# The scaling of row maxima to biases, moved from ScalarE to GpSimd in 29 of 32 head pairs

## What is computed

```python
h = _layernorm(x, axis=-1) * (1 + ca) + sa
x = x + ga * _L0_attn_ref(h, wq, wk, wv, wo)
h = _layernorm(x, axis=-1) * (1 + cb) + sb
x = x + gb * _L0_ffn_ref(h, W_base, b_base, W_gate, W_thr, b_thr, A_w, B_w)
```

```python
scores = jnp.einsum('bqhd,bkhd->bhqk', q, k) * scale
scores = jnp.where(causal[None, None], scores, jnp.finfo(scores.dtype).min)
probs = jax.nn.softmax(scores, axis=-1)
out = jnp.einsum('bhqk,bkhd->bqhd', probs, v).reshape(b, s, d)
```

## Time and profile before

| | us |
|---|---|
| median of 3 runs | 1601.21 (1600.83 to 1603.35) |
| the profiled execution | 1600.5 |
| its span | 1598.7 |
| granted TensorE clock over the span | 0.987 of 2.4 GHz |
| TensorE busy | 1539.8 |
| ScalarE busy | 1039.8 |
| VectorE busy | 934.7 |
| GpSimd busy | 605.6 |

### The profile page before, as it was taken

One profiled execution on the slowest core, in us unless ns is written; L12 is line 12 of the kernel. 1 busy time (PEld: TensorE's weight loads), 2 busy tenths in 40 slices (PEclk: granted clock), 3 DMA queues, 4 the chain that ended last, 5 costly groups with the idle time before them and its releaser, 6 DMA issues. The chain is left out here.

```text
span 1598.7 us, 29576 instructions
## 1 busy us (share of the span) xinstructions
PE 1539.8 (96%) x9578; PEld 1209.3 (76%) x9578; DVE 934.7 (58%) x2900; ACT 1039.8 (65%) x2718; POOL 605.6 (38%) x477
## 2 busy tenths in 40 slices
PE   5899999999999999999999999998989999999996
PEld 3667777777777777777777777775669989999996
DVE  4727576576665656666657566666654545454544
ACT  2548899999999988999899899988631111110100
POOL 3334253443533324235243243337114343434342
PEclk9999999999999999999999999997999999999999
DMA  9783444445542393243333432444341212122110
GB/s 344 273 261 86 107 108 108 123 114 142 131 117 74 86 304 83 66 99 74 95 74 81 107 81 61 97 143 120 120 119 40 79 41 77 50 70 63 55 66 27
DMA packets 172035, 174.44 MB, mean 109 GB/s; under 512 B 21044, under 2 KB 120676, under 8 KB 171896
## 3 DMA queue, kind: packets, MB, share of 16 engines
q1 hardware_dynamic: 169784, 168.54, 38.0%
q10 hardware_dynamic: 2112, 4.19, 0.7%
HBM read 96.65 MB, written 25.18 MB: 76 GB/s over the span
## 5 line engine op out<-in xcount | busy, mean ns | idle before, releaser
L1584 ACT ACTIVATE rows_sb<-rows_sb,bias_m 128x640 f32<-128x640 f32 (+7 forms) x512 | 396.0, 774 | 12.5
L1854 DVE CUSTOM_DVE_ANT_0 rows_sb<-ps_t,mask 128x512 f32<-128x512 f32 (+3 forms) x512 | 297.4, 586 | 162.7 <-PE ps_t L1313 155.5
L1313 PE MATMUL ps_t<-stk 96*128 96x512 f32 (+3 forms) x768 | 268.6, 352 | 5.1 <-DMA stk<-rot 1.7
L1620 ACT ACTIVATE probsT<-ps_s 128x512 f32<-128x512 f32 (+1 forms) x488 | 243.2, 536 | 33.3 <-PE ps_s L1344 17.3
L1344 PE MATMUL ps_s<-stk 98*128 98x512 f32 (+3 forms) x768 | 222.7, 371 | 1.0 <-DMA stk<-m_rows 1.0
L1880 DVE TENSOR_TENSOR ps_s<-ps_s,mask_t 128x128 f32<-128x128 f32 (+1 forms) x384 | 120.8, 341 | 166.3 <-PE ps_s L1344 162.7
L1313 PEld LDWEIGHTS ps_t<-stk 96*128 96x128 f32 x768 | 146.0, 190 | 51.9 <-DVE m_rows L1870 9.6
L2016 POOL TENSOR_TENSOR rope_b<-rope_b,rope_sin 128x512 f32<-128x512 f32 x64 | 82.8, 1293 | 267.6 <-DVE rope_b L1839 267.6
L1344 PEld LDWEIGHTS ps_s<-stk 98*128 98x128 f32 x768 | 132.2, 191 | 66.4 <-issue 30.2
L1854 DVE CUSTOM_DVE_ANT_0 rows_sb<-ps_t,mask,smax_part 128x128 f32<-128x128 f32 (+3 forms) x256 | 140.8, 550 | 39.4 <-PE ps_t L1313 11.9
L1300 PE MATMUL ps_qkv<-hT_hi,w_hi 128*128 128x512 f32 x384 | 158.2, 412 | 3.9 <-DVE hT_lo L1823 3.9
(11 more groups left out here) (222 smaller groups left out, 3179.8 us busy)
## 6 DMA issues: line engine op xcount, KB each, us to landing
stk<-rot SPq DMA_DIRECT2D x384, 128.0 KB, 2.4
probsT<-in_L_wmod_dram SPq DMA_DIRECT2D x5, 2048.0 KB, 9.0
wm_one<-in_L_wmod_dram SPq DMA_DIRECT2D x5, 2048.0 KB, 11.5
w_raw<-in_L_attn_wq_dram SPq DMA_DIRECT2D x16, 512.0 KB, 3.9
w_raw<-in_L_attn_wk_dram SPq DMA_DIRECT2D x16, 512.0 KB, 4.7
w_raw<-in_L_attn_wv_dram SPq DMA_DIRECT2D x16, 512.0 KB, 4.1
attn_scratch<-attn_sb SPq DMA_DIRECT2D x128, 64.0 KB, 3.0
h_scratch<-h_pair SPq DMA_DIRECT2D x32, 256.0 KB, 3.1
```

Of the source, the lines that this page charges most:

```text
L1313: pe.matmul(bank[:, 0:c1 - c0], stk[0:3 * HD, u % 2, 0, qt // 4, h, qt % 4 * P:(qt % 4 + 1) * P], stk[0:3 * HD, u % 2, 1, part, h, 0:c1 - ...
L1584: act.activation(row, row, ACT.Exp, bias=bias_m[:, qt, h:h + 1], scale=SCALE, accum_out=sums[:, qt // 4, h, qt % 4:qt % 4 + 1]).then_inc(s ...
L1620: act.activation(probs[PROBS[w]][:, hs[0]:hs[-1] + 1, 0:n], s_bank[(NS * u + k) % 3][:, 0:len(hs) * n].rearrange("p (h n) -> p h n", h=len ...
L1854: dve.tensor_tensor_reduce(rows_sb[:, to, at + c0:at + c1], bank[:, 0:n], mask[:, BANK - n:BANK] if last else mask[:, 0:1].broadcast_to([P ...
```

## The change

From pair 1 to pair 29 (that is, the rows computed one pair ahead, in pairs 0 to 28) GpSimd computes the biases, at the beginning of the slot in which ScalarE uses them, ahead of GpSimd's other work of that slot. ScalarE keeps its waits for max_ok and bias_ok and drops the operation. GpSimd waits for max_ok, and for sum_ok of the pair before, whose exponentials read the same bias. Pairs 0, 30 and 31 stay as they were.

```diff
--- before.py
+++ after.py
@@ -1576,7 +1576,8 @@
                     both = w if qt >= 4 else w + 1
                     hs = slice(h, h + 1) if qt >= 4 else slice(0, 2)
                     act.wait_ge(max_ok, NR * u + ENDS[both] + 1)
-                    act.mul(bias_m[:, qt, hs], smax[:, u % 2, qt // 4, hs, qt % 4], -SCALE).then_inc(bias_ok, 1)
+                    if u == 0 or u >= PAIRS - 2:
+                        act.mul(bias_m[:, qt, hs], smax[:, u % 2, qt // 4, hs, qt % 4], -SCALE).then_inc(bias_ok, 1)
                 act.wait_ge(bias_ok, NB * u + bias_no(w) + 1)
                 if w in (0, EARLY_WHOLE) and u:
                     act.wait_ge(log_ok, 2 * (u - 1) + w // EARLY_WHOLE + 1)
@@ -1980,6 +1981,20 @@
                 pool.wait_ge(pool_ve, n + 1)
                 pool.tensor_tensor(rstd[:, tt % 2:tt % 2 + 1], vareps[:, :], minus_half[:, :], ALU.pow).then_inc(ln_rs, 1)
 
+            def biases(u, i):
+
+                if u >= PAIRS - 2:
+                    return
+                for w in EXPS.get(i, ()):
+                    qt, h = WHOLE[w]
+                    if qt >= 4 or not h:
+                        both = w if qt >= 4 else w + 1
+                        hs = slice(h, h + 1) if qt >= 4 else slice(0, 2)
+                        pool.wait_ge(max_ok, NR * u + ENDS[both] + 1)
+                        pool.wait_ge(sum_ok, NW * (u - 1) + both + 1)
+                        pool.tensor_scalar(bias_m[:, qt, hs], smax[:, u % 2, qt // 4, hs, qt % 4], -SCALE, None,
+                                           ALU.mult).then_inc(bias_ok, 1)
+
             def next_rest(tt, half):
                 pool.wait_ge(ln_hi, 2 * (NT + tt) + half + 1)
                 pool.tensor_tensor(h_next.bitcast(F32R), h_next, h_next_hi,
@@ -2060,6 +2075,7 @@
             for u in range(PAIRS):
                 t, p = u // 2, u % 2
                 for i in range(NU):
+                    biases(u + 1, i)
                     if (u, i) in ROUND_AT:
                         rest_rot(*ROUND_AT[u, i])
                     step = norm_step(u, i)
```

## The result

The changed kernel takes 1939.66 us (median of 5 runs, 1936.29 to 1949.12) against 1600.83 us beside it (5 runs). The ratio is 1.2119, with a 95% interval of 1.2100 to 1.2137: 21% slower. The forecast was 1940. The profiled execution is the slowest of the five, 1949.12 us with a span of 1947.3, so sums are made against a difference of 348.6 us of span.

A forecast was written before the change was run, and what follows sets the result against it. The prediction took ScalarE and TensorE, both nearly full, to hold each other up. Stalls from GpSimd's queue added 318 us to 1600.5, giving 1919; 21 us for TensorE's clock made 1940, range 1800 to 2080.

The forecast's parts named there:

- The order on GpSimd: GpSimd works in order, so biases queued behind its rotations and remainders come late and ScalarE waits: 18.5 us per even pair.
- The places: Slots where ScalarE would wait for a late bias: 2, 3, 4, 6, 8, 9, 10, 11 of even pairs; 3, 6, 9 of odd.
- The link, 1.5 us: Bias queued behind a GpSimd remainder that waits for ScalarE's split or rounding: 2.28 us to the next exponential instead of 0.75.
- Slots 6 and 9, moving along with X through the three score banks: Even pairs: late ScalarE delays TensorE's score banks, hence the rotation ahead of the bias; lateness reaches 10.8, then 15.2 us.
- X: ScalarE's lateness against the earlier trace, followed through an even pair's slots; forecast to reach 18.5 us in slot 11.
- Odd pair, 3.1 us: Stalls in odd pairs' slots 3, 6 and 9, together 7.2 us, less 2.1 for biases in time and 2.0 of older waits.
- Sum: 15 even pairs x 18.5 plus 14 odd x 3.1, less 2: +318 us on 1600.5, giving 1919 before the clock.
- The clock, 21 us: TensorE, less busy, runs partly at half clock; at most 190 us over all pairs, of which a ninth was taken.
- Rival 3: TensorE's clock falls for good: up to 190 us instead of 21, so up to 2109 us; chance 0.15.
- Price of an operation: GpSimd's bias operation takes 0.19 us, from 128x1 additions, with 0.66 kept for the range; SBUF conflicts count nothing in the sum.
- rival 1: GpSimd answers in time; ScalarE gets 80 us back and TensorE's waits shrink by 24 us: 1576 us; chance 0.03.
- The signs to look for: Profile signs: ScalarE's bias_m wait longest, 250 to 350 us in about 300 waits; even pairs about 50 us, odd 34 to 36.

## Why the prediction was right

- **The order on GpSimd** was the cause, shown by the kernel with one slot's shift, which takes back 300 of 339 us.
- **The places**: all eleven forecast stalls occurred. Besides them stand only four waits of 0.7 to 1.4 us, in slot 2 of the odd pairs 3 to 9, which are among those in which the second batch is normalized.
- **The link, 1.5 us**: from the split's start to the next exponential it is 1036.14 - 1033.90 = 2.24 us, where 2.28 was forecast and 0.75 stood before, so a link cost 1.49. The idle times of 1.62 to 1.67 in the rows are longer, since they also hold the place of the bias that ScalarE made itself before.
- **Slots 6 and 9, moving along with X through the three score banks**: shown in TensorE's wait of 3.53 us in slot 5. Mis-sized on the low side: in the table X steps by 4.9 and 4.5 us, where 4.1 and 3.1 were forecast. Over pairs 12 to 27 the steps are 4.7 and 4.3, and with TensorE kept busy 4.0 and 3.3: nearly all of the gap is the clock, which the sum has as a term of its own.
- **Odd pair, 3.1 us**: measured 3.7. Over pairs 12 to 27 the steps of X in slots 3, 6 and 9 make 7.6 us for the 7.2 forecast (5.0 in slot 9 for 4.7), nine biases in time give back 2.1 as forecast, and older waits 1.8 for 2.0. They closed less since two waits for values grew instead (1.81 and 1.82 us in pair 21, where they were 0.77 and 0.52). TensorE was granted 0.61 from 1074 to 1083 us, just there, but that this is the reason is not shown: with TensorE kept busy the two waits and the odd pair's 3.7 stayed, and the clock at that place was still only 0.81.
- **Sum**: 15 x 20.5 + 14 x 3.7 = 359 by the pairs measured against 348.6 of span; 318 + 21 were forecast. The outer pairs grew less than those of the middle: pairs 0 and 1 together 19.8 us, 10 and 11 together 21.0, pair 28 16.5, and pairs 2 to 9, in which the second batch is normalized, 11.8 a pair for 12.1. I had taken all pairs as alike. This error and the low terms above nearly cancel, so that a forecast within 1 us of 1939.66 is in part luck.
- **The clock, 21 us**: 20 to 24 were taken back by keeping TensorE busy. The mechanism and its small size are right, but the ninth of 190 us that I took was a guess that no row gave, and that it came out is luck. Rival 3, a fall for good, did not come: 0.90 and not 0.5 granted. TensorE: Matmul & The Clock Gate of the Trainium skill (part 1) says that the clock is set by how busy TensorE has recently been. The trace agrees (0.90 at 163 of 200 us busy, 1.00 at 200 of 200).
- **Price of an operation**: the row of 128x1 additions (0.191) was a near neighbour; the bias took 0.211. Its longest, 0.718, was rare: four of the 348 took over 0.4 us. The GPSIMD Engine Reference of the Trainium skill (Specifications) tells of a conflict with VectorE over the shared SBUF interface. The median shows no sign of it, as the sum had taken; whether the four long ones are such a conflict no run here shows.
- **Wrong in what it rested on**: rival 1's worth of ScalarE's time. I gave a gain of 24 us to biases that come in time. With 86 and 142 of them moved it is nothing, with 303 and 348 minus 4. The statement that ScalarE and TensorE "hold each other up, both nearly full" was half true: a longer ScalarE holds TensorE up (though only 1.4 us of the odd pair's 4.8 came through when that stall stood nearly alone), a shorter one does not release it.
- **The signs to look for** did not follow from my own terms. "About 300 waits": the eleven places make 15 x 8 + 14 x 3 = 162, and 161 were recorded. "250 to 350 us" of wait for bias_m: it was 429.5. The waits must first make up for the 348 x 0.23 = 80 us that ScalarE no longer works, and for the older waits that close, 15 x 0.6 + 14 x 2.0 = 37; with the 318 of the sum that is 435. Even pairs took 52 us for "about 50", odd ones 36.
- Two slips in the working carry no weight. 31.8 of 50 us is 64%, not 62%. And of the 0.6 us "counted above" among the waits for values and maxima 0.27 was a gap without a named releaser, which is not among those waits.

What stays open: what holds TensorE up in the waits without a named releaser, about 56 us in the attention before the change; no run here touched them. The worth of the clock beyond 0.968 was not tried.

## What to carry to other kernels

Before moving a small operation to an idle engine, look at what stands ahead of it in that engine's order at the moment when it is wanted, not at the engine's busy share: GpSimd was 38% busy, and its 1.3 us operations stood exactly there. Everything behind the waiting instruction pays the stall, here eight times in an even pair. And do not book a freed microsecond on the second-busiest engine as a gain: here 20 to 80 us of ScalarE's work were taken away and no time was won. Try the cheapest version (here VectorE's) before tuning the place.

## What was not expected of the hardware

The granted clock fell in the attention, where TensorE's longest gap was 3.7 us: within pairs 20 and 21 it was 0.88, with TensorE busy 73.69 of 89 us. Within these pairs it changed from stretch to stretch: 0.70 from 1042 to 1050 us, behind the gap of 3.53 us, and 0.61 from 1074 to 1083, with 1.00 from 1083 to 1095 behind it. The kernel before was granted 1.00 from 130 to 1090 us. VectorE makes the bias in 154 ns, ScalarE in 204, GpSimd in 211: the 57 ns between them are small beside the stalls of 1.2 to 5.5 us that GpSimd's queue made.
